# Output chunks of the feed-forward product in two row tiles of 64 rows, alone in units 1, 5, 9 and 13

## What is computed

```python
h = gamma1 * rmsnorm(x) + beta1                    # per item, from cond
a = softmax(scale * q(h) @ k(h).T) @ v(h)          # 16 heads of 16
x = x + alpha1 * (a @ W_o.T)
h = gamma2 * rmsnorm(x) + beta2
x = x + alpha2 * (silu(h @ gate_w.T) * (h @ hidden_w.T) @ out_w.T + out_b)   # hidden 1024
out = (layernorm(x) * w + b + tanh(cond @ lin_w.T + lin_b)) * w + b
```

## Time and profile before

| | before |
|---|---|
| runs | 753.05, 753.93, 753.97 us, median 753.93 |
| profiled execution | 755.2 us, span 753.4 us |
| busy: PE, DVE, ACT, POOL | 95%, 71%, 62%, 52% of the span |
| mean granted TensorE clock | 0.988 |
| reductions of maxima (L1174) | 256.8 us |
| exponentials (L967) | 223.6 us |

### The profile page before, as it was taken

The page is one execution under the profiler, slowest core; times in us unless marked ns, Lnnn a source line. Parts: engine busy times, 40 slices in busy tenths (PEclk is TensorE's granted clock), DMA queues, the critical chain, the costliest instruction groups (busy, mean ns, idle before and its releaser), DMA issues.

```text
span 753.4 us, 17410 instructions
## 1 busy us (share of the span) xinstructions
PE 712.2 (95%) x6660; PEld 501.2 (67%) x6660; DVE 532.9 (71%) x797; ACT 467.1 (62%) x860; POOL 391.6 (52%) x493
## 2 busy tenths in 40 slices
PE   6698999899999999999999999999999999999995
PEld 5343444467777677767677667767777667679895
DVE  4787787777677767777677767777677766336765
ACT  4467777775667657675666666775666655753431
POOL 4365143552378625865367533866257544872533
PEclk9889999999999999999999999999999999999998
DMA  7677557456434635274453654264354620331210
GB/s 228 169 236 247 194 172 266 121 165 207 151 96 144 191 133 170 63 228 140 143 151 107 207 155 155 60 192 162 99 171 127 178 81 3 90 92 64 54 48 29
DMA packets 63275, 107.17 MB, mean 142 GB/s; under 512 B 10480, under 2 KB 18344, under 8 KB 63192
## 3 DMA queue, kind: packets, MB, share of 16 engines
q1 hardware_dynamic: 61892, 104.66, 45.6%
q10 hardware_dynamic: 1172, 1.20, 0.6%
q0 software_dynamic: 128, 0.20, 0.1%
HBM read 57.50 MB, written 37.52 MB: 126 GB/s over the span
## 4 chain that ended last, share of the span: by engine, by line
PE 66%; DMA 8%; DVE 7%; issue 6%; POOL 5%; ACT 5%; SPq 2%; ACTq 0%; POOLq 0%; DVEq 0%
PE ps_x L1483 15%; PE ps_o L1459 12%; PE ps_j L1354 10%; PE ps_o L1496 9%; PE ps_s L1443 7%; PE ps_m L1424 6%; DVE mx L1174 3%; ACT prob L967 2%; DMA d_c<-reciprocal_scratch 2%; DMA reciprocal_scratch<-d_s 2%; DMA out_scratch<-o_raw 1%; DMA stack_scratch<-qk_hi 1%; PE ps_m L1483 1%; PE ps_s L1483 1%; DMA n_x<-n 1%
## 5 line engine op out<-in xcount | busy, mean ns | idle before, releaser
L1174 DVE TENSOR_REDUCE mx<-ps_m 128x2 f32<-128x1024 f32 x211 | 256.8, 1217 | 49.1 <-PE ps_m L1424 48.8
L967 ACT ACTIVATE prob<-ps_s 128x1024 f32<-128x1024 f32 x219 | 223.6, 1021 | 45.8 <-PE ps_s L1443 44.1
L1459 PE MATMUL ps_o<-prob,v 128*32 128x512 f32 x1024 | 127.5, 600 | 0.1
L1443 PE MATMUL ps_s<-qs,ks 64*128 64x512 f32 x438 | 101.3, 457 | 7.8 <-issue 4.0
L674 POOL TENSOR_TENSOR a_lo<-act_y,a_hi 128x256 fp32r<-128x256 f32 x100 | 73.6, 736 | 62.1 <-ACT a_hi L1000 62.0
L1424 PE MATMUL ps_m<-ks,qs 64*128 64x512 f32 x422 | 90.7, 424 | 9.2 <-DVE mx L1174 5.5
L1483 PE MATMUL ps_x<-n_x,gh_hi 64*128 64x256 f32 x872 | 97.2, 280 | 0.7 <-DMA n_x<-n 0.7
L1215 DVE SCALAR_TENSOR_TENSOR act_y<-act_y,ps_x 128x256 f32<-128x256 f32 x109 | 45.8, 420 | 73.1 <-ACT act_y L993 73.1
L1483 PE MATMUL ps_x<-n,gh_hi 64*128 64x256 f32 x872 | 97.0, 280 | 0.0
L1443 PEld LDWEIGHTS ps_s<-qs,ks 64*128 64x128 f32 x438 | 41.6, 184 | 76.7 <-issue 50.5
L1483 PEld LDWEIGHTS ps_x<-n,gh_hi 64*128 64x128 f32 x872 | 76.0, 186 | 2.6 <-issue 0.2
(11 more groups left out here) (182 smaller groups left out, 1476.3 us busy)
## 6 DMA issues: line engine op xcount, KB each, us to landing
qs<-stack_scratch SPq DMA_DIRECT2D x30, 512.0 KB, 4.7
ks<-stack_scratch SPq DMA_DIRECT2D x30, 512.0 KB, 6.3
stack_scratch<-qk_hi SPq DMA_DIRECT2D x56, 256.0 KB, 3.6
out_scratch<-o_raw SPq DMA_DIRECT2D x32, 256.0 KB, 2.3
n_x<-n SPq DMA_DIRECT2D x32, 256.0 KB, 3.7
stack_scratch<-qk_lo SPq DMA_DIRECT2D x28, 256.0 KB, 3.9
on_lo<-out_scratch SPq DMA_DIRECT2D x16, 256.0 KB
d_c<-reciprocal_scratch SPq DMA_DIRECT2D x16, 256.0 KB
```

The costliest lines, as they stand in the source:

```text
L967: act.activation(prob[:, n % 3, 2 * h:2 * h + 2, :], score_pair(n, h)[:], ACT.Exp, scale=SCALE).then_inc(p_r, 1)
L1174: dve.tensor_reduce(mx[:, group % 2, :, h, qt], max_pair(mp)[:], AX.X, ALU.max).then_inc(mx_red, 1)
L1443: mm = pe.matmul(score_pair(n, j)[:, s, :], ks[r:r + 64, g, j, kb * P:(kb + 1) * P], qs[r:r + 64, g, j, :], start=True, stop=True)
L1459: mm = pe.matmul(ps_o[32 * i:32 * i + 32, :], v[:, at:at + 32], prob[:, n % 3, i, :], start=(kb == 0), stop=(kb == TT - 1), skip_group_che ...
```

## The change

The chunks of 4 steps stay in units 1, 5, 9 and 13. Each of its 24 products is now made as two matmuls of 64 rows, the upper rows into `ps_o`, the lower ones into `ps_j` (`ps_f`, `ps_f2`), and no other job or attention stands in these units. The jobs of the table move: Q and MT from 1 to 2 and 5 to 6, FT(0) from 9 to 10, FT(1) from 13 to 14, MT(3) from 9 to 8, MT(0) from 13 to 12; K and V of units 3 and 4 change places. The first job of a unit comes ahead of the attention, the second behind it. In the unit after a chunk, ScalarE copies `ps_o` to `sc` ahead of its exponentials (`top_tile`), VectorE adds `ps_j` after its first reduction (`sum_tiles`), and gate and scaling follow the second reduction. The first job, the next attention group and so on wait for the sum (`f_sum_r`). On POOL a_low comes ahead of the chunk's addition, n2_low of FT(0) in unit 11 and not 10, as does its swap on SP, where stack writes move too.

```diff
-          5: (("Q", 1, 1), ("MT", 2, 0)), 7: (("WO", 0, -1),), 8: (("WO", 1, -1),), 9: (("FT", 0, -1), ("MT", 3, 0)),
+          6: (("MT", 2, 0), ("Q", 1, 1)), 7: (("WO", 0, -1),), 8: (("WO", 1, -1), ("MT", 3, 0)), 10: (("FT", 0, -1),),
-TURN = {GH_AT: [("V", 1, 2)], GH_AT + 1: [("MT", 0, 2)], GH_AT + 2: [("K", 1, 2)], GH_AT + 6: [("FT", 1, 0)]}
+TURN = {GH_AT: [("V", 1, 2)], GH_AT + 1: [("MT", 0, 2)], GH_AT + 2: [("K", 1, 2)],
+        GH_AT + 4: [("TR", 1, 3), ("FT", 1, 0)]}
...
-        ps_f = ps_o[:].rearrange("p (t n) -> p t n", t=2)
+        ps_f, ps_f2 = (bank[:].rearrange("p (t n) -> p t n", t=2) for bank in (ps_o, ps_j))
...
-                if at(10, -1):
+                if at(11 if GH_AT <= n < NU else 10, -1):
                     swap_halves(b - 1, 0)
...
-                if at(10, -1) and n < NU:
+                if at(11 if n >= GH_AT else 10, -1) and n < NU:
                     n2_low(b - 1, 0)
...
+                if 0 <= e < TAIL:
+                    a_low(e)
                 if chunk_at(n - 1) is not None:
                     add_to_x(("F", chunk_at(n - 1)))
-                if 0 <= e < TAIL:
-                    a_low(e)
...
+            def top_tile(c):
+
+                if SC_NO["F", c] > 1:
+                    act.wait_ge(x_add, SC_NO["F", c] - 1)
+                act.wait_ge(f_done, CH * (c + 1))
+                act.activation(sc[:], ps_f, ACT.Copy).then_inc(f_top_r, 1)
...
+                if chunk_at(n - 1) is not None:
+                    top_tile(chunk_at(n - 1))
                 if n < NU:
                     exps(n, 0)
...
+            def sum_tiles(c):
+
+                dve.wait_ge(f_top_r, c + 1)
+                dve.tensor_tensor(sc[:], ps_f2, sc[:], ALU.add).then_inc(f_sum_r, 1)
...
+                if what[0] == "F":
+                    dve.wait_ge(f_sum_r, what[1] + 1)
+                    dve.wait_ge(tab_f_in, 16 * ((CH * (what[1] + 1) - 1) // (2 * JC) + 1))
+                    dve.tensor_tensor(sc[:], sc[:], factor, ALU.mult).then_inc(sc_r, 1)
+                    return
...
                 for m, mp in enumerate(maxima_at(n)):
                     reduce_max(mp)
+                    if m == 0 and late:
+                        sum_tiles(chunk_at(n - 1))
                     if mp == LEAD_IN:
                         evac(("TR", 0, 1), n)
-                    if m == 0 and 0 <= e < TAIL:
+                    if m == late and 0 <= e < TAIL:
+                        if late and jobs_at(n)[:1] and jobs_at(n)[0][0] == "MT":
+                            evac(jobs_at(n)[0], n)
                         gate(e)
...
+                if late:
+                    scale(("F", chunk_at(n - 1)))
+                if GH_AT <= n < NU and at(2, -1):
+                    o_recip(b - 1, 1)
                 if at(10, -2):
                     statistics(b - 2, 0)
...
                 for e in range(CH * c, CH * c + CH):
-                    project_out(e, ps_f, e == CH * c, e == CH * c + CH - 1)
+                    pe.wait_ge(a_lo_r, e + 1)
+                    for t in range(2):
+                        for m, (a, o) in enumerate(PARTS):
+                            for r, bank in enumerate((ps_f, ps_f2)):
+                                rows = slice(64 * r, 64 * r + 64)
+                                mm = pe.matmul(bank[:, t, :], A[a][rows, e % RING, t * P:(t + 1) * P],
+                                               OW[o][rows, e % JC, :], start=(e == CH * c and m == 0 and t == 0),
+                                               stop=(e == CH * c + CH - 1 and m == 2), skip_group_check=True)
+                    mm.then_inc(f_done, 1)
...
-                for what in order_at(n):
-                    if what[0] == "F":
-                        project_chunk(what[1])
-                    else:
-                        job(what)
-                for d in attended_at(n):
+                if chunk_at(n) is not None:
+                    job_evacuated(last[0])
+                    project_chunk(chunk_at(n))
+                    last[0] = ("F", chunk_at(n))
+                jobs, units = jobs_at(n), attended_at(n)
+                for what in jobs[:1]:
+                    job(what)
+                for d in units:
                     attend(d)
+                for what in jobs[1:]:
+                    job(what)
```

More of the change, by code:

```diff
@@ L96, in chunk_at @@
     return c if n >= CHUNK_AT and (n - CHUNK_AT) % CH == 0 and c < CHUNKS else None
[L99 to L103, removed]
 SC = sorted([(CHUNK_AT + CH * c, 0, ("F", c)) for c in range(CHUNKS)]
@@ L527, in unit @@
                     max_rows(b, 1)
-                if at(2, 1) and n >= GH_AT:
-                    stack_write(b + 1, 0)
                 if n == UNITS + 2:
@@ L534, in unit @@
                     rec_write(b - 1, 1)
-                    if ("FT", 1, 0) in jobs_at(n - 1):
+                    if b == 2:
                         swap_halves(0, 1)
+                if at(3, 1) and n >= GH_AT:
+                    stack_write(b + 1, 0)
+                if at(3, -1) and b > 1:
                     rec_read(b - 1, 1)
@@ L546, in unit @@
                     load_xr(0, 1)
[L547 to L550, removed]
                 if at(4, 0):
                     o_write(b, 0)
+                if at(5, 1):
+                    stack_write(b + 1, 1)
                 if at(7, 1) and n < GH_AT:
@@ L1300, in unit @@
                     scale(("H", 2 * (b - 2) + 1))
+                if late and not maxima_at(n):
+                    sum_tiles(chunk_at(n - 1))
                 if 0 <= e < TAIL and not maxima_at(n):
+                    if late and jobs_at(n)[:1] and jobs_at(n)[0][0] == "MT":
+                        evac(jobs_at(n)[0], n)
                     gate(e)
+                if late:
+                    scale(("F", chunk_at(n - 1)))
+                if GH_AT <= n < NU and at(2, -1):
+                    o_recip(b - 1, 1)
                 if at(10, -2):
@@ L1306, in unit @@
                     statistics(b - 3, 1)
-                for what in order_at(n) if n < NU else []:
-                    if what[0] == "F":
-                        scale(what)
-                    else:
+                for what in jobs_at(n) if n < NU else []:
+                    if not (late and what[0] == "MT"):
                         evac(what, n)
-                if at(3 if b == 1 else 2, -1):
+                if at(3 if b == 1 else 2, -1) and not GH_AT <= n < NU:
                     o_recip(b - 1, 1)
@@ L1344, in job_evacuated @@
                     pe.wait_ge(m_lo_r, NG * b + i + 1)
-                elif kind in ("WO", "F"):
+                elif kind == "WO":
                     pe.wait_ge(sc_r, SC_NO[job])
+                elif kind == "F":
+                    pe.wait_ge(f_sum_r, job[1] + 1)
                 elif kind == "FT":
```

27 lines of the change are left out of this document (12 added, 15 removed).

## The result

The changed kernel takes 777.69 us (median of 4 runs, 773.24 to 781.51), the kernel before 753.70 in the same comparison: a ratio of 1.031, 95% interval [1.028, 1.0341]. I had said 767, with a range up to 777. The direction was right, the size was not: 24 us against 13. The profiled execution took 778.62 us with a span of 776.8, 23.4 us over the span before. The runs also spread over 8 us, where those before lay within 1 (within 4 in the later comparisons).

The account below looks back on a forecast made before the run. TensorE, busy for 95% of the span, was taken as the bound, with VectorE next. Terms came to +2.4 us a round, +14 over six, less 1: 768 profiled, 767 us as median, range 752 to 777.

Parts of the forecast that it names:

- The SP moves: SP's queue: stack writes a unit later, two behind a read, costed at nothing with readers three to four units off.
- Max rows are made a unit later for two groups: Rows of the maxima for two groups: made a unit later, still landing 3 us ahead of use.
- Switches: TensorE's changes between 64-row and 128-row work: fewer of them, -0.3 us a round, -1.9 over six rounds.
- The wait for the sum: First job after a chunk waits for VectorE's sum: +0.6 us a round in units 2, 6 and 14.
- FT(0), "the largest term": FT(0) moved to unit 10: its chain makes n_x late, TensorE waiting 2.25 us a round in units 11 and 12.
- Q at the end of units 2 and 6: Q's evacuation delays the next unit's second maxima by 0.45 us; unit 4 regains 0.3; net about nothing.
- Last round: FT(0)'s chain in the last round: copy and swap sooner, but unit 11 short, so about as much waiting.
- What goes: FT(1, 0) moves from unit 34 to 32: a 0.95 us wait goes, unit 33 is delayed about 0.9, nothing left.
- Sum without the failed step: Whole kernel: +2.4 us a round, six rounds +14, less 1 for the shorter last one.
- VectorE did not keep up: Rival that VectorE and DMA keep up, so no FT(0) chain wait: 749 to 753 us or somewhat slower; chance 0.2.
- the clock's rival: Waits in units 11 and 12 lower TensorE's clock: 1.5 us each round, +9 more in six, 776 us; chance 0.12.

Follow-up runs that it names:

- the first experiment: Changed kernel with the swap of FT(1) moved on SyncE behind the loads and stack read, ahead of the output write: 765.67 us, ratio 1.0157.
- the last experiment: The run with a_low first, but every chunk as one product over all 128 rows: 767.03 us, ratio 1.0176 to the kernel before.
- the run with a_low first: Changed kernel with FT(1)'s swap later, FT(0) evacuated first, unit 10's statistics in unit 11, and a_low ahead of moments and normalisation there: 763.55 us, ratio 1.012.

## Why the prediction was wrong

**The step that failed is one sentence**: "The SP moves (stack writes a unit later, two behind a read) I cost at nothing: their readers are three to four units off", with the one behind it, "Max rows are made a unit later for two groups and still land 3 us ahead of use". The readers of the moved writes were indeed in no trouble. I had left out a move that the diff doesn't show: the swap of FT(1) goes with its job, onto another unit of SP's queue, ahead of five loads that had been gone 10 us earlier. I followed FT(0) engine by engine and FT(1) not at all, since its reader is four units off. The runs put that step at 12 us: it is the whole difference between 778 and the 765.7 that is left without it, which my 767 meets within 1.5 us. That it is met so closely is partly luck, as the terms below were off both ways. The move made the swap late twice: with its job it went a unit on, and on POOL its low part then stood behind a wait of 2.40 us for the chunk's scaling. I priced the DMA issues by who reads them, never by what stands in the DMA queues ahead of a transfer that something waits for.

**The terms, one by one.**
- *Switches.* Unit 9 of a round 5.30 (said 5.34), FT alone 0.59 (0.58), MT alone 0.21, Q 1.59 (1.60): right. The edge from the attention to a job that I took from rows 3 isn't there. That the tiling by itself gains nothing was right for a pair of half tiles inside (2.82 us for 24), but too hard on the whole: 0.2 us of the product's edges and 0.1 of the maxima come back per chunk, 0.7 us a round by the last experiment.
- *The wait for the sum.* Said 0.6 a round; in units 2, 6 and 14 the job starts 0.38 us after the last maxima instead of 0.33, and FT in unit 10 starts 2.54 into it (said 2.65): 0.2 at most.
- *FT(0), "the largest term".* Said 2.25. Units 11 and 12 grew by 0.93 and 1.03, together 1.96, with the order of events as forecast. Right, 0.3 too much. In unit 92 n_x was 1.2 us later than that.
- *Q at the end of units 2 and 6.* Said: a delay of 0.45 each in the units behind them, 0.3 back in unit 4, about nothing in all. Units 51 and 55 grew by 0.46 and 0.49, units 52 and 56 lost 0.48 and 0.10: 0.4 a round.
- *Last round.* "About as much": unit 124 went from 5.60 to 8.94, 3.3 us. The short units 121 to 123 give the chain no cover.
- *What goes.* The wait of rows 7 went: unit 36 lost 1.25 us, where unit 52 of the next round lost 0.48. Unit 33 lost 1.02 where unit 49 lost 1.81, so the delay of about 0.9 that I had given it is there too, 0.8. But unit 32 grew by 1.88, since FT(1, 0) waits there 1.19 us for the evacuation of TR ahead of it, and that I had at nothing. Units 32 and 33 together grew by 0.85.
- *Sum without the failed step.* Said +13; the profile of the first experiment has +10.9 between units 28 and 127, its runs +11.4.

**The rivals.** VectorE did not keep up, and the waits of 0.77 us each left the clock alone in every round, so that the clock's rival had the wrong place. That its 776 lies near the measured time is luck: the 12 us are the late write's. But after the stalls of the failed step and of unit 124 the clock did fall. Stretches after the stall of unit 67, in the changed kernel:

```profile
357.00:360.00 3.00, 1.39 (x14) 0.83 (x10) 2.93 (x6) 1.33 (x3) 0.73 (x1) 1.00 0.67 186
360.00:364.00 4.00, 3.68 (x27) 3.20 (x27) 1.86 (x2) 1.91 (x3) 0.00 (x0) 0.59 0.72 250
```

PE waited 1.61 us in the first of these, and in the second the products ran on average at 0.59 of the clock. In the tail the product with W_o waits 2.40 us for on_lo, behind the same late denominators, and slows in the same way:

```profile
711.76 0.36 PE L1377 MATMUL ps_j<-wo_hi,on_hi 128*128 128x256 f32 x1 [2.40 <-POOL on_lo L680]
...
712.55 0.42 PE L1377 MATMUL ps_j<-wo_lo,on_hi 128*128 128x256 f32 x1
```

With the swap later the wait there is 0.58 us. This is why the late write costs more than the waits that it makes.

**Shown, and left open.** Shown by edits that do one thing: the swap's place costs 12 us; the loads ahead of the write make its landing late, and neither the held queue nor the place of the reciprocal does; the chain from FT(0) makes the waits for n_x; the tiles gain 4 us once their surroundings are mended. Not settled: why the remaining 8.5 us resist. By the profile of the run with a_low first, the middle rounds have 0.4 us each of it, units 32 and 33 0.85, the round from 97 1.3 and units 113 to 126 3.3, though its unit 116 was 1.5 us shorter than before the change; the tail is level. Only argued, from the traces: that the write landed sooner with whole chunks because the swap went out 2.4 us earlier.

## What to carry to other kernels

When a job moves, list the DMA waits that move with it on the issuing queue, and then everything that stands behind them: here a blocked queue released five loads in one burst, and the next transfer that a chain hung on paid for them. Putting the swap that waits for a slow engine behind loads that were ready gave 12 us; putting the write ahead of the loads gave 6, as the loads then held the read. And mend one late chain at a time: a gain in one unit was given back at another queue in five of these runs.

## What the runs showed of the hardware

- The issue of the write of o_raw on SP mostly takes 0.33 us and took 3.05 behind five loads; the write then landed 11.2 us after, against 2.0 for that of another group 48 us later in the same kernel. With the loads behind it, it landed after 2.2 us in the same turn, and the read behind the loads took 9.1 us instead of 2.0 in another.
- The clock doesn't follow the last wait alone. The waits of 0.77 us in units 11 and 12 never lowered it, and behind those of 0.79 and 1.97 us in units 91 and 92 it stayed at 1.00 as well; one of 1.61, and 1.25 with 1.89 two microseconds behind, were followed by 0.59 and 0.50. And unit 116 has one and the same pair of waits in most runs (0.97 to 1.04 us for the exponentials, 0.55 for the maxima): before the change the gate behind them took 2.56 us (its clock in the earlier trace rows), with FT(0) of unit 122 ahead 2.40, with the swap later 1.43. What decides between these, no run here shows.
- A chunk of 24 products takes 2.82 us as pairs of half tiles between 64-row work, and 3.02 as full products in the same place.
